# A two-layer graph network on one core: where the adjacency matrix's rows wait, who sums its columns, and which engine scales g

## What is computed

```python
h = relu(layernorm(x))
support = relu(quant_act(h) @ quant_weight(weight))      # 4-bit and 3-bit levels
x1 = x + adj @ quant_act(support)                        # layer 0
g = relu(layernorm(x1))
A = (adj + adj.T) * 0.5 + I
dinv = A.sum(axis=1) ** -0.5
out = x1 + adj @ (dinv[:, None] * A * dinv[None, :]) @ g
```

## Time and profile before

| | us |
|---|---|
| median of 3 runs | 557.7 (555.09 to 557.93) |
| the profiled execution's own time | 555.93 |
| its span, first to last instruction | 553.9 |
| TensorE busy | 516.5 |
| VectorE busy | 264.5 |
| ScalarE busy | 149.4 |
| GpSimd busy | 90.0 |
| mean granted TensorE clock | 0.984 of full |

### The profile page before, as it was taken

The page is one execution under the profiler, slowest core; times in us unless marked ns, Lnnn a source line. Parts: engine busy times, 40 slices in busy tenths (PEclk is TensorE's granted clock), DMA queues, the critical chain, the costliest instruction groups (busy, mean ns, idle before and its releaser), DMA issues.

```text
span 553.9 us, 6745 instructions
## 1 busy us (share of the span) xinstructions
PE 516.5 (93%) x2552; PEld 258.0 (47%) x2552; DVE 264.5 (48%) x392; ACT 149.4 (27%) x206; POOL 90.0 (16%) x56
## 2 busy tenths in 40 slices
PE   2867699999999969999997999999999999999997
PEld 2745355555555624444442444444444444444443
DVE  4996225444354496888889877764000000000000
ACT  1687745444553221232334212214000000000000
POOL 0134599855540000000000000000000000000000
PEclk9999979999999889999998999999999999999999
DMA  6900175544442213223233223300801001001001
GB/s 245 363 0 2 48 243 178 172 148 143 153 141 101 64 57 115 76 76 114 79 111 114 77 91 99 114 0 25 298 20 38 19 19 38 19 19 38 19 19 38
DMA packets 19251, 51.64 MB, mean 93 GB/s; under 512 B 2336, under 2 KB 2336, under 8 KB 19232
## 3 DMA queue, kind: packets, MB, share of 16 engines
q1 hardware_dynamic: 18656, 51.39, 27.7%
q10 hardware_dynamic: 576, 0.00, 0.1%
HBM read 42.99 MB, written 8.39 MB: 93 GB/s over the span
## 4 chain that ended last, share of the span: by engine, by line
PE 81%; DVE 11%; ACT 3%; DMA 2%; issue 2%; POOL 1%; SPq 0%; ACTq 0%; DVEq 0%
PE ps_a L909 30%; PE ps_p L798 18%; PE ps_a L872 6%; PE ps_b L872 6%; PE ps_p L872 6%; PE ps_a L785 3%; PE ps_m L872 3%; PE ps_h L872 3%; PE ps_b L785 2%; DVE split L677 2%; PE ps_b L762 2%; DVE a_in L668 2%; ACT split L423 2%; DVE a_in L667 1%; DMA feat<-in_x 1%
## 5 line engine op out<-in xcount | busy, mean ns | idle before, releaser
L798 PE MATMUL ps_p<-small,at 128*128 128x512 f16 x512 | 120.5, 390 | 5.0 <-DVE feat L610 5.0
L909 PE MATMUL ps_a<-small,at 128*128 128x512 f16 x384 | 85.5, 379 | 0.0
L909 PE MATMUL ps_a<-a_in,at 128*128 128x512 f16 x384 | 85.5, 379 | 0.0
L734 DVE SCALAR_TENSOR_TENSOR feat<-ps_a,feat 128x512 f32<-128x512 f32 x16 | 11.1, 691 | 153.8 <-PE ps_a L909 153.8
L798 PEld LDWEIGHTS ps_p<-small,at 128*128 128x128 f16 x512 | 51.4, 101 | 62.8 <-issue 6.5
L423 ACT ACTIVATE split<-a_in 128x1024 f16<-128x1024 f32 x32 | 33.8, 1057 | 131.1 <-PE ps_p L872 63.7
L909 PEld LDWEIGHTS ps_a<-small,at 128*128 (+1 forms) x384 | 37.6, 98 | 45.3
L909 PEld LDWEIGHTS ps_a<-a_in,at 128*128 (+1 forms) x384 | 37.6, 98 | 45.3
L677 DVE TENSOR_TENSOR split<-a_in,split 128x1024 f16<-128x1024 f32 x32 | 39.2, 1224 | 33.6 <-ACT split L423 33.6
L307 POOL TENSOR_TENSOR at<-at,a_in 128x1024 f32<-128x1024 f32 x20 | 46.8, 2353 | 17.8 <-DMA a_in<-in_adj 17.8
L872 PE MATMUL ps_a<-feat,split 128*128 (+1 forms) x180 | 44.8, 386 | 4.9 <-DVE small L681 3.2
(11 more groups left out here) (124 smaller groups left out, 449.0 us busy)
## 6 DMA issues: line engine op xcount, KB each, us to landing
a_in<-in_adj SPq DMA_DIRECT2D x54, 512.0 KB, 3.8
out<-feat SPq DMA_DIRECT2D x32, 256.0 KB, 2.0
split<-in_adj SPq DMA_DIRECT2D x10, 512.0 KB, 4.2
feat<-in_x SPq DMA_DIRECT2D x8, 512.0 KB, 10.4
feat<-out SPq DMA_DIRECT2D x4, 1024.0 KB, 9.6
at<-in_L_gnn_weight SPq DMA_DIRECT2D x2, 512.0 KB, 5.8
scal<-in_L_gnn_act_alpha ACTq DMA_DIRECT2D x2, 0.5 KB, 6.8
scal<-L_gnn_adj_scaling_factor ACTq DMA_DIRECT2D x1, 0.5 KB, 3.8
```

The costliest lines, as they stand in the source:

```text
L734: nc.vector.scalar_tensor_tensor(xr, BANK[t % 2], 1.0 / (SA * SZ), xr, ALU.mult, ALU.add)\
L798: last = nc.tensor.matmul(l0_bank(r), at_block(r, lo, j), small[:, j * D:(j + 1) * D], start=(j == 0 and lo == 0), stop=(j == T - 1 and lo ...
L909: last = nc.tensor.matmul(BANK[n], at_block(t, lo, j), z_part(j, z_lo), start=(j == 0 and lo + z_lo == 0), stop=(j == T - 1 and lo == 1))
```

## The change

Seven edits, in the order of the program:

1. The first 14 units instead of 6 are loaded at once (`AHEAD`). Units 6 to 13 go into the store's tiles 15, 9, 8 and 7, which are idle then; later units go round the same six slots as before, and there is a semaphore for each of the 14. A slot is free when its unit is turned and row-summed.
2. GpSimd's column sums, the 16 small products on TensorE and all waits for them are gone.
3. VectorE sums each turned unit's columns out of PSUM (`column_sum`, a tensor_reduce of 8 x 128 elements per partition to 8), between ScalarE's high part and its own low part, for units 6 to 31. For units 0 to 5 it sums the two stored 16-bit parts later (`column_sum_late`, 2048 elements per partition to 8), one in each of the first six tiles of layer 0.
4. ScalarE's row sums of units 0 to 5 are spread over its list: two before each high part of units 6 to 11.
5. Tiles 14 and 15 of layer 0 are accumulated in `ps_h` and `ps_m`, and no longer wait for the `x1_tile` of two tiles before. Sweep 0's first step now waits for four `x1_tile`s, in the order of the banks: tiles 14, 15, 12, 13.
6. `g_tile` is one ScalarE instruction (clip of scale times x plus shift), with `late_shift` from VectorE; `g_low` is a plain subtraction.
7. VectorE's list between the stages is put in another order.

```diff
-            for u in range(RING, 2 * RING):
-                rows_again(u)
-            for r in range(10):
-                rows_again(2 * r + 2 * RING)
-                rows_again(2 * r + 2 * RING + 1)
-                store_x1(r)
...
+            for u in range(AHEAD):
                 rows(u)
+            for u in range(AHEAD, UNITS):
                 rows_again(u)
+                if u % 2 and u >= 17:
+                    store_x1((u - 17) // 2)
...
         def l0_bank(r):
+            if r >= 14:
+                return (ps_h, ps_m)[r - 14][:, :]
             return ps_p[:, (r % 2) * D:(r % 2 + 1) * D]
...
+            def column_sum(u):
+
+                dve.wait_ge(athi, u + 1)
+                nc.vector.tensor_reduce(colp[:, u * B:(u + 1) * B],
+                                        turn_bank(u)[:, :].rearrange("p (b i) -> p b i", i=P), AXIS.X, ALU.add)
+
+            def column_sum_late(u):
+
+                both = at4[:, u // 2, :, (u % 2) * W:(u % 2 + 1) * W].rearrange("p two (b i) -> p b two i", i=P)
+                nc.vector.tensor_reduce(colp[:, u * B:(u + 1) * B], both, AXIS.XY, ALU.add)
...
             for r in range(12):
+                column_sum(2 * r + EARLY)
                 lo_turned(2 * r + EARLY)
                 x1_tile(r)
+                if r < EARLY:
+                    column_sum_late(r)
+                column_sum(2 * r + EARLY + 1)
                 lo_turned(2 * r + EARLY + 1)
...
+            def g_tile(t):
+
+                act.wait_ge(late_ready, 1 + (t >= LATE_GROUPS[1]) + (t >= LATE_GROUPS[2]))
+                if t >= 2:
+                    act.wait_ge(g_ready, t - 1)
+                nc.scalar.activation(tmp[:, (t % 2) * D:(t % 2 + 1) * D], feat[:, t * D:(t + 1) * D], ACT.Relu,
+                                     bias=late_shift[:, t:t + 1], scale=rd[:, t:t + 1]).then_inc(gt_ready, 1)
...
-                if r == 13:
-                    pe.wait_ge(acc_done, UNITS)
-                    for k in range(T):
-                        last = nc.tensor.matmul(ps_m[:, k:k + 1], acc[:, k * P:(k + 1) * P], mean_of[:, 0:1],
-                                                start=True, stop=True)
-                    last.then_inc(col_ps, 1)
...
-                            if t >= 6:
-                                pe.wait_ge(x1_ready, t + 9)
+                            if t >= 4:
+                                pe.wait_ge(x1_ready, (15, 16, 13, 14)[t - 4])
```

More of the change, by code:

```diff
@@ L17 @@
 EARLY = 6
+AHEAD = 14
 ACT_LEVELS = 2 ** 4 - 1
@@ L79, in gnn_kernel @@
         wstat = sb("wstat", 4)
+        colp = sb("colp", UNITS * B)
+        late_shift = sb("late_shift", T)
+        cols = sb("cols", T)
         def late(tile, off, cols, dt):
@@ L84, in late @@
             return v.bitcast(f32) if dt == f32 else v
-        acc = late(15, 0, N, f32)
         w_raw = late(14, 0, KD * D, f32)
@@ L121, in gnn_kernel @@
         x_in = [sem(f"x_in{n}") for n in range(T // 2)]
-        a_arr = [sem(f"a_arr{k}") for k in range(RING)]
+        a_arr = [sem(f"a_arr{k}") for k in range(AHEAD)]
         s_arr = [sem(f"s_arr{k}") for k in range(4)]
@@ L157, in gnn_kernel @@
         ghi = sem("ghi")
+        late_ready = sem("late_ready")
         g_ready = sem("g_ready")
@@ L176, in unit_in, with before @@
         def unit_in(u):
-            k = u % RING
+            if EARLY <= u < AHEAD:
+                tile = (15, 9, 8, 7)[(u - EARLY) // 2]
+                return late(tile, u % 2 * 2 * W, W, f32)
+            k = u % RING if u < EARLY else (u - AHEAD) % RING
             return a_in[:, k * W:(k + 1) * W] if k < 4 else splitf[:, (k - 4) * W:(k - 3) * W]
+        def before(u):
+            return u - AHEAD if u < AHEAD + RING else u - RING
         SLOT = (2, 3, 0, 1)
+        LAST_USER = [max(u for u in range(AHEAD, UNITS) if (u - AHEAD) % RING == k) for k in SLOT]
         def sum_in(v):
@@ L298, in support_out @@
                                         ALU.add, ALU.mult).then_inc(sq_ready, 1)
-            def accumulate(u):
-                half = acc[:, (u % 2) * W:(u % 2 + 1) * W]
-                pool.wait_ge(a_arr[u % RING], arrivals(u))
-                if u < 2:
-                    nc.gpsimd.tensor_scalar(half, unit_in(u), 0.0, 1.0, ALU.add, ALU.mult).then_inc(acc_done, 1)
-                else:
-                    pool.wait_ge(acc_done, u - 1)
-                    nc.gpsimd.tensor_tensor(half, half, unit_in(u), ALU.add).then_inc(acc_done, 1)
             for n in range(T // 2):
@@ L314, in _ @@
                 support_out(m)
-            for u in range(UNITS):
-                accumulate(u)
         @block.scalar
@@ L400, in _ @@
             scale_support(7)
-            for u in range(EARLY):
-                row_sum(u)
             for u in range(EARLY, UNITS):
-                row_sum(u)
-                if u == UNITS - 2:
-                    act.wait_ge(col_ps, 1)
+                if u < 2 * EARLY:
+                    row_sum(2 * (u - EARLY))
+                    row_sum(2 * (u - EARLY) + 1)
+                else:
+                    row_sum(u)
                 hi_turned(u)
@@ L429, in _ @@
             late_root(0)
-            act.wait_ge(acc_done, UNITS)
+            g_tile(0)
             sum_hi(0)
             g_hi(0)
+            g_tile(1)
             sum_hi(1)
             g_hi(1)
+            late_root(1)
+            g_tile(2)
             g_hi(2)
-            late_root(1)
+            late_root(2)
             for v in range(2, T):
+                if v + 1 < T:
+                    g_tile(v + 1)
                 sum_hi(v)
@@ L684, in _ @@
             sum_unit(0)
-            g_tile(0)
+            x1_tile(13)
             sum_lo(0)
@@ L688, in _ @@
             sum_unit(1)
-            x1_tile(13)
-            g_tile(1)
+            x1_tile(14)
+            late_var(1)
             sum_lo(1)
             g_low(1)
+            late_scale(1)
             sum_unit(2)
-            g_tile(2)
-            x1_tile(14)
-            late_var(1)
-            g_low(2)
-            g_tile(3)
             x1_tile(15)
             late_var(2)
+            g_low(2)
+            late_scale(2)
             sum_lo(2)
             g_low(3)
-            late_scale(1)
-            sum_unit(3)
-            g_tile(4)
-            sum_lo(3)
-            g_low(4)
-            late_scale(2)
-            for v in range(4, T):
+            for v in range(3, T):
                 sum_unit(v)
-                if v + 1 < T:
-                    g_tile(v + 1)
                 sum_lo(v)
```

62 lines of the change are left out of this document (29 added, 33 removed).

## The result

The changed kernel takes 541.5 us (median of four runs, 541.0 to 542.0) against 556.5 for the kernel before in the same series (555.1 to 557.9). The ratio is 0.973, with an interval of 0.970 to 0.977. The forecast was 542.0 with a range of 538.5 to 549.5. The profiled execution took 541.03 us, of which 538.9 are the span. That span is 15.0 us shorter than before.

The account below looks back on a forecast made before the run. TensorE, 93% busy, was taken to lose time to waits and low clock, with VectorE pacing sweep 0. Layer 0's 18.83 us became 14.8 by step 15: 541.1 from the profile, 542.9 from the median; forecast 542.0, range 538.5 to 549.5.

Parts of the forecast that it names:

- own banks: Layer 0, tiles 14 and 15: removes a 4.96 us wait for an `x1_tile` and 1.65 us of low clock.
- VectorE's reserve after six tiles: Layer 0: VectorE's margin before TensorE needs a bank shrinks from 2.0 us by 0.35 per tile to 0.2.
- stop at `ps_m`: First step of sweep 0: TensorE newly waits 4.4 us, from 195.04 until 199.5, for `x1_tile(15)`.
- low clock behind it, first step: Sweep 0: slow TensorE clock after its wait for `x1_tile(15)` costs 1.65 us; the first step ends at 203.1.
- low part of step 2: Sweep 0: VectorE starts this piece at 204.2, 1.17 us after TensorE's first step ends.
- step 15 earlier by: End of sweep 0: VectorE's low part comes 15.1 us earlier, 14.2 if low clock lasts; 14.8 taken.
- The tile time of VectorE: Layer 0: one of VectorE's first six tiles lasts 9.0 us against TensorE's 8.65, afterwards 6.5.
- my formula: Layer 0: TensorE loses 6 x (D - 4.55) - 2.0 us, D pricing two column sums and a late one.
- The rival of dearer reductions: Layer 0: VectorE's reductions cost a fifth or so more, TensorE loses up to 6.1 us, total 548; chance 0.12.
- No new wait: Start of sweep 0: `x1_tile(15)` is over in time, TensorE doesn't stop, 1.7 us more gain, 540; chance 0.04.
- The opening is not longer: Opening: rival that early loads get in the way, up to 6.6 us late, total 548; chance 0.06.
- the gain did not vanish: Whole kernel: rival that waits move to something unseen and nothing is gained, 556 to 558; chance 0.04.

Follow-up runs that it names:

- The repeated reductions: Changed kernel with all six late column sums of 2048 elements formed a second time into an unread buffer; 550.88 us, ratio 0.991.
- one of them: Changed kernel with only the first tile's late column sum formed a second time; 541.95 us, ratio 0.975.
- the repeat: The changed kernel measured once more, unaltered, as base of the first group of experiments; 541.74 us, ratio 0.975 against the kernel before.
- the column-sum run: Kernel before without TensorE's column-sum products and the waits for them, degrees from row sums alone; 549.90 us, ratio 0.989.

## Why the prediction was right

The mechanism held at each place it named, but for the worth of the own banks.

| step | predicted | measured |
|---|---|---|
| turn 6 / turn 31 start (chain) | 65.50 / 173.67 | 65.54 / 173.71 |
| layer 0 ends | 191.80 | 191.69 (191.85 as the chain counts, and the prediction with it) |
| reductions, 1024 and 2048 elements | 1.22, 2.44 | 1.22, 2.25 |
| VectorE's reserve after six tiles | 0.2 | about 2.6 |
| `sum_unit(0)` starts | 182.3 | 181.94 |
| `x1_tile(15)` frees `ps_m` | 199.5 | 198.97 |
| stop at `ps_m` | 4.4 | 3.94 |
| low clock behind it, first step | 1.65 | 2.1 |
| low part of step 2 | 204.2 | 204.23 |
| periods of sweep 0 | 5.68, 5.34 | 5.67, 5.34 |
| idle before a low part | 1.2 | 1.12 |
| step 15 earlier by | 14.8 | 15.05 |

Four things in it were off or unsaid.

*The tile time of VectorE.* The sum had 9.0 us for one of the first six tiles. The work in it is 8.39 (8.66 less 0.26 of idle time, with rounding). The late sum took 2.25 and not 2.44. And instructions that wait for nothing start 1.13 to 1.14 us after one another although each is shown as 1.21 us long (73.56 and 74.69), where I had added 1.22 and 1.25. So the reserve did not shrink to 0.2 us: VectorE waits for ScalarE once per tile and unit 7's low part has 2.6 us to spare. The repeated reductions confirm it from the other side: 9.1 to 9.4 us lost where my formula gave 14.8 (12.5 with the measured durations), and nothing for one of them. The rival of dearer reductions rested on the thin reserve and was further off than I thought.

*Two errors that cancel.* The stop was 0.5 us shorter than said and the low clock behind it 0.45 longer. The low part of step 2 came out right within 0.03 us because of that, which is luck: in the repeat the low clock cost 0.4 us more in the step behind, and step 15 came 0.5 us later.

*The own banks.* The sum gives them 6.61 of layer 0's 18.83 us. Alone on the kernel before they end layer 0 5.69 us earlier and the kernel not at all. In the changed kernel they shorten layer 0 by 0.6 us and lengthen the whole by 2.6. The second wait goes either way: with the shared banks it is 0.53 and not 4.96 us, because `x1_tile(13)` moved ahead of `sum_unit(1)`, an edit to which the sum gives nothing. That this place is the cause is read from the lists and from the column-sum run, where the wait stayed at 4.20; no run moved it alone. The prediction followed the path to step 2 as a whole, so its sum did not suffer. But it listed this edit among the gains and did not see that the same path is shorter without it: the own banks put the wait for `x1_tile(15)` six products earlier in the first step.

*No new wait.* I priced this rival at 540. With `x1_tile(15)` early it is real and measures 539.0, with VectorE's low part at 202.16 where I had 202.5. What was underestimated is the clock after the stop: 0.5 us more behind the first step.

The other rivals fell. The opening is not longer (turn 6 at its wanted 65.54); TensorE never waits for a low part in layer 0; and the gain did not vanish.

The reductions agree with the rule that was weighed (the Trainium skill, "VectorE: DVE Perf Modes", perf-mode tier table): 1024 elements took 1.22 us in 32 bits and 2048 took 2.25 in 16 bits, 1.19 and 1.10 ns per element, so the shorter type did not bring a second element per step. The rule's advice to avoid the operation does not decide here, since it ran beside TensorE.

## What to carry to other kernels

A wait removed is worth only what its whole path to the next common point gains: follow it to the first instruction that another engine sets, as here the low part of step 2, and price each edit by taking it out of the finished kernel too, since one that gains 5.7 us locally in the old kernel can cost 2.6 in the new one. When the resource behind a stop comes free at a fixed time, let the waiting engine meet it as late in its list as it can. An engine that idles once per period before its critical instruction wants its next independent work moved ahead of that wait; here that gave 0.65 us by step 15 on its own, and 6.2 us together with the shared banks, tiles 13 and 15 of `x1_tile` earlier and the late scales later.
